# First attention of a fused mLSTM-attention and fp4 feed-forward kernel: the next unit's second score half and state sums issued ahead of this unit's values

## The chip, the cores and the metric

The kernel runs on one core of a Trainium2 chip. The metric is the device time of one execution in microseconds. Before the change it is 559.58 us, the median of 3 runs (558.65 to 561.35).

## What is computed

An attention with gated decay (mLSTM) and a residual, then a feed-forward layer with fp4 weights and a residual, on x of 8 batches x 256 tokens x 512 features. Cut to what matters:

```python
# attention, for each of 8 batches and 16 heads of width 32 (q = layernorm(x), k = v = ctx)
ig, fg   = concat(q, k, v) @ Wi + bi, concat(q, k, v) @ Wf + bf      # per token and head
log_D    = tril(cumsum differences of log_sigmoid(fg)) + ig
D        = exp(log_D - rowmax(log_D))
C        = (q @ k.T / sqrt(32)) * D
h        = C / (max(|rowsum(C)|, exp(-rowmax)) + eps) @ v
x        = x + headwise_layernorm(h) * ln_scale

# feed-forward: gate and up 512 -> 2 x 1408, down 1408 -> 512, fp4 weights with scales
y        = silu(ln(x) @ w_gate) * (ln(x) @ w_up) @ w_down
x        = x + y / rms(y)
```

## The kernel before

The 8 batches are worked in 4 pairs `p`. Attention of pair `p` shares its stretch of the program with the feed-forward layer of pair `p - 1` (`q`). The first pair has no feed-forward beside it (`q is None`); this is **the first attention**, and in it DVE unpacks the fp4 weights (`decode`, a chain of three operations on DVE) and ACT widens them (`convert`). The first attention is all that the change touches.

Attention of a pair is cut into 8 units (`UNITS`): 4 groups of 4 heads by 2 batches. For unit `u` the work is this:

- ACT, `exps(p, u, half)`: 8 exponentials write the decay matrix `dmat[:, u % 2]`. They wait for `pv_done` of unit u - 2, since that unit's values have read the same buffer.
- POOL, `mask(p, u)`: two triangular selects on `dmat`, one for each half of the exponentials, then two small products that write `vw[:, u % 2]` (values weighted by the last row's decay) and count `vw_ready`.
- PE, `scores(p, q, u, 0)` and `(..., 1)`: q k.T in two halves, into banks of `pq` for even units and of `pf` for odd ones.
- PE, `state_sums`: one product of the context with `vw`, the state that the first 128 tokens hand to the later 128. It waits for `vw_ready` of its unit.
- DVE, `products`: scores times `dmat`, in place. It waits for the whole scores, the mask and `vw`. Then `keep_state` copies the state sums out.
- PE, `values(p, q, u)`: 8 small products of `dmat` with `v_sb` into `po`, then one product of `state` with the queries into the second part of bank `pq[:, 1]`, which counts `pv_done`.
- ACT `read_o` copies `po` out, DVE `later_part` scales the part that came from the state, and `add_later` adds it.

In the first attention PE also runs identity matmuls of 128x512 that nothing reads, `keep_busy(count)`, beside its units.

Each engine has a program of its own, written as a loop over 22 steps `h`, and runs it strictly in order. What sets the order is a table: unit u has its scores step at h = 2u + 1 and its values step at h = 2u + 2. At the values step of unit u PE runs, in the first attention, `scores(u + 1, 0)`, `keep_busy`, `values(u)`, `scores(u + 1, 1)`, `state_sums(u + 1)`, `keep_busy`. On ACT, step 2u + 3 holds `read_o(u)` and then `exps(u + 2)`; on POOL it holds `mask(u + 2)`.

After the last unit come the head norm, the first residual and the second layer norm, mostly one chain on DVE, and then the feed-forward layer of the first pair.

Semaphore waits are written ahead of the operation that they guard, as `pe.wait_ge(...)`; everything behind such a wait on that engine waits too.

Of the kernel before, what the change touches and what calls it, by code (L numbers as in the profile page):

```python
# [32 lines left out]
P = 128  # L33
B, S, E, NH = 8, 256, 512, 16
DH = E // NH
# [3 lines left out]
HG = P // DH  # L39
# [70 lines left out]
def xattn_ffn(nc, x, ctx, ctxT, w_gates, b_gates, ln_scale, gu_bytes, gu_scales, dn_bytes, dn_scales, out):  # L110
# [7 lines left out]
    with es:  # L118
# [98 lines left out]

        def bank_qk(p, u, half):
            return pf[:, 2 * half] if p == 0 and u % 2 else pq[:, 2 * half]

        def bank_y(p, n):
            return po[:] if n == 2 else pq[:, min(n, 2)]
# [573 lines left out]
        def _(pe):  # L796
# [71 lines left out]
            def state_sums(p, q, u):  # L868

                hg, b = u // 2, u % 2  # L870
                pe.wait_ge(vw_ready, 2 * UNITS * p + 2 * u + 2)
                if u > 0:
                    pe.wait_ge(later_ready, UNITS * p + u)
                elif q is not None:
                    pe.wait_ge(t_ready, 4 * FT * q + 2)
                pe.matmul(pq[:, 1, 0:HG * (DH + 1)], ctx_sb[:, 2 * b, hg * P:(hg + 1) * P],  # L876
                          vw[:, u % 2].rearrange("q h d -> q (h d)"), start=True, stop=True
                          ).then_inc(st_done, 1)

            def values(p, q, u):  # L880
                hg, b = u // 2, u % 2
                if u == 0 and q is not None:
                    pe.wait_ge(acc_ready, 4 * FT * q + 2)
                if u == 0:
                    pe.wait_ge(v_ready, TT * p + TT)
                if u > 0:
                    pe.wait_ge(o_read, UNITS * p + u)
                elif not (isinstance(p, int) and p == 0):
                    pe.wait_ge(o_read, UNITS * p)
                for half in range(2):  # L890

                    pe.wait_ge(prod_done, 2 * UNITS * p + 2 * u + 1 + half)
                    for s in range(BLKS):
                        for hh in range(2):
                            h = 2 * half + hh
                            pe.matmul(po[:, (s * HG + h) * (DH + 1):(s * HG + h + 1) * (DH + 1)],  # L896
                                      dmat[:, u % 2, half, s, hh], v_sb[:, 2 * b + s, hg * HG + h],
                                      start=True, stop=True)

                pe.wait_ge(state_ready, UNITS * p + u + 1)  # L900
                pe.matmul(pq[:, 1, HG * (DH + 1):2 * HG * (DH + 1)], xT[:, hg, b * S + P:(b + 1) * S],  # L901
                          state[:, u % 2].rearrange("q h d -> q (h d)"), start=True, stop=True
                          ).then_inc(pv_done, 1)
# [73 lines left out]
            def keep_busy(count):  # L977

                words = ident[:].bitcast(F16)
                for _ in range(count):  # L980
                    pe.matmul(pf[:, 3], words[:, 0:P], words.unsqueeze(1).to_broadcast([P, 2, 2 * P]),  # L981
                              start=True, stop=True)

            def iteration(p, q, n):
                for h in range(GU):
                    if q is not None:
                        ffn_up(q, h)
                    if p is not None:

                        s = slot(q, h)  # L990
                        if q is None and s in VALUES and VALUES[s] + 1 < UNITS:
                            scores(p, q, VALUES[s] + 1, 0)
                            keep_busy(6 if VALUES[s] == 0 else 3)
                        if s in VALUES:
                            values(p, q, VALUES[s])
                            if q is None and VALUES[s] + 1 < UNITS:
                                scores(p, q, VALUES[s] + 1, 1)
                                state_sums(p, q, VALUES[s] + 1)
                                keep_busy(6 if VALUES[s] == 0 else 3)
                        if s in SCORES and (q is not None or SCORES[s] == 0):  # L1000
                            scores(p, q, SCORES[s], 0)
                            if q is None:
                                keep_busy(16)
                            state_sums(p, q, SCORES[s])
                            scores(p, q, SCORES[s], 1)
                if q is not None:
                    down(q, 0, range(FT))
                    down(q, 1, range(FT))
                if n is not None:
                    if q is None:  # L1010
                        keep_busy(16)
                    turn_x(n)
                    gate_sums(n)
                    if q is None:
                        keep_busy(36)
                if q is not None:
                    down(q, 2, range(FT))
                if p is not None:
                    turn_y(p)
                if q is not None:  # L1020
                    down(q, 3, range(FT - 3))
                if n is not None:
                    turn_back(n)
                if q is not None:
                    down(q, 3, range(FT - 3, FT))
# [14 lines left out]
        def _(dve):  # L1040
# [87 lines left out]

            def keep_state(p, u):
                dve.wait_ge(st_done, UNITS * p + u + 1)  # L1130
                dve.tensor_tensor(state[:, u % 2], pq[:, 1, 0:HG * (DH + 1)].rearrange(
                    "q (h d) -> q h d", h=HG), own_rows[:], ALU.mult).then_inc(state_ready, 1)

            def later_part(p, u):
# [155 lines left out]
            def iteration(p, q, n):  # L1290
                for h in range(GU):
                    s = slot(q, h)
                    u = SCORES.get(s) if p is not None else None
                    if u is not None and q is None:
                        products(p, u, range(BLKS))
                        keep_state(p, u)
                    if q is not None:
                        ffn_up(q, h, p, u)
                        if q == 0 and h % 2 == 0:
                            down_weights(h // 2)  # L1300
                        if h % 2 == 1 and h > 1:
                            gate(q, h // 2 - 1)
                    elif h in WORDS_AT:
                        i = WORDS_AT[h]
                        decode_up(i) if i < UP_CHUNKS else decode_down(i - UP_CHUNKS)
                    if p is not None and s in VALUES:
                        later_part(p, VALUES[s])
                    if p is not None and s in ADD:
                        add_later(p, ADD[s])
                    if q is None and 11 <= h < 11 + TT:  # L1310
                        norm1_sums(n, (h - 11,))
                    if q is None and h == 11 + TT:
                        shift1(n)
# [97 lines left out]
```

## Time and profile before

| | us |
|---|---|
| median of 3 runs | 559.58 |
| lowest and highest | 558.65, 561.35 |
| the profiled execution, device time | 560.9 |
| its span, first to last instruction | 559.2 |
| PE busy in the span | 504.4 (90%) |
| DVE busy | 391.4 (70%) |
| POOL busy | 331.9 (59%) |
| ACT busy | 295.6 (53%) |

The span is 1.7 us shorter than the device time of that execution. The eight units of the first attention lie between about 42 and 89 us of the span. The values of unit 0 begin at 45.05 us and those of units 1 to 7 at 52.69, 57.81, 62.93, 68.05, 73.17, 78.96 and 84.46 us; the last product of unit 7 ends at 88.57 us. Times in timelines are counted from the start of the span. The granted clock of TensorE is shown as a share of full speed: 1.00 is 2.4 GHz and 0.50 is 1.2 GHz.

### The profile page before, as it was taken

To read this page: it belongs to the slowest core of one execution; us is meant where nothing else is said; L and a number is where in the kernel's file an instruction comes from. 1 tells how busy PE (TensorE), PEld (TensorE's weight loads), DVE (VectorE), ACT (ScalarE), POOL (GpSimd) and SP (SyncE) were. 2 spreads that over 40 slices of the span, in tenths; PEclk is the share of its full clock that TensorE was granted. 3 is DMA by queue.
4 is the path that set the end of the run, shared out by engine and by line. 5 is a ranking of instruction groups with operands and counts; after the bars stand their busy time and mean duration, and the time that the engine had idled before them with its cause. 6 is when DMAs were issued, how large, how long until landed. Compare 5 with 4: busy or idle time off the path is not lost.

```text
span 559.2 us, 8167 instructions
## 1 busy us (share of the span) xinstructions
PE 504.4 (90%) x2728; PEld 279.4 (50%) x2728; DVE 391.4 (70%) x691; ACT 295.6 (53%) x639; POOL 331.9 (59%) x371
## 2 busy tenths in 40 slices
PE   0449989968999899999999999999999989988996
PEld 0326765425666444456665445466664443322442
DVE  4675886985888897647777899377778962877301
ACT  0335765275777623377786354577766123866000
POOL 1043533457888685466777783767777662888501
PEclk9868996988999999999999999999999999999999
DMA  8654309164200600166006000653000000200000
GB/s 254 174 156 186 114 2 320 38 227 151 77 1 2 226 1 1 42 222 240 28 2 226 1 0 4 198 212 119 2 0 2 19 20 19 94 1 1 19 20 38
DMA packets 22218, 48.33 MB, mean 86 GB/s; under 512 B 1824, under 2 KB 8864, under 8 KB 21536
## 3 DMA queue, kind: packets, MB, share of 16 engines
q1 hardware_dynamic: 22176, 47.81, 25.4%
q8 instruction: 22, 0.36, 0.3%
q14 instruction: 20, 0.16, 0.1%
HBM read 37.84 MB, written 4.33 MB: 75 GB/s over the span
## 4 chain that ended last, share of the span: by engine, by line
PE 68%; DVE 14%; issue 5%; ACT 4%; POOL 4%; DMA 4%; SPq 1%; DVEq 0%; POOLq 0%; ACTq 0%
PE pf L972 25%; PE pf L958 17%; PE po L896 9%; PE pq L864 6%; PE pq L876 2%; DMA ts<-in_gate_up_bytes 2%; DVE ffn L1221 2%; PE pq L958 2%; PE pq L901 2%; ACT dmat L648 2%; PE pf L981 2%; DVE ffn L1225 1%; PE pq L826 1%; POOL hT L530 1%; ACT ts L682 1%
## 5 line engine op out<-in xcount | busy, mean ns | idle before, releaser
L972 PE MATMUL pf<-w_down,hT 128*128 128x512 f32 x352 | 154.1, 595 | 1.7 <-DVE w_down L1287 1.7
L958 PE MATMUL pf<-yT,gu_val 128*128 128x512 f16 x552 | 135.6, 385 | 4.2 <-ACT th L707 1.5
L525 POOL TENSOR_TENSOR ffn<-ffn,ts 128x512 f32<-128x512 f32 x88 | 117.6, 1337 | 31.9 <-DVE ffn L1225 22.1
L682 ACT ACTIVATE ts<-pf,gu_scale 128x512 f32<-128x512 f32 x138 | 87.5, 684 | 51.1 <-PE pf L958 50.8
L972 PEld LDWEIGHTS pf<-w_down,hT 128*128 128x128 f32 x352 | 65.9, 190 | 83.7 <-issue 77.1
L958 PEld LDWEIGHTS pf<-yT,gu_val 128*128 128x128 f16 x552 | 50.7, 99 | 68.7 <-DVE ffn L1225 8.2
L648 ACT ACTIVATE dmat<-negm,aT 128x128 f32<-128x128 f32 x256 | 80.0, 395 | 4.9 <-DMA negm<-negm_dram 4.9
L530 POOL TENSOR_TENSOR hT<-ffn,th 128x512 f32<-128x512 f32 x44 | 57.6, 1313 | 30.9 <-DVE th L1234 30.9
L1221 DVE SCALAR_TENSOR_TENSOR ffn<-pf,gu_scale,ts 128x512 f32<-128x512 f32 x69 | 51.6, 748 | 33.7 <-PE pf L958 20.0
L896 PEld LDWEIGHTS po<-v_sb,dmat 128*128 128x128 f32 x512 | 64.2, 197 | 5.3 <-issue 0.9
L486 POOL TENSOR_SCALAR_AFFINE_SELECT dmat<-dmat 128x512 f32<-128x512 f32 x64 | 44.2, 704 | 30.7 <-ACT dmat L648 30.7
L896 PE MATMUL po<-v_sb,dmat 128*128 128x33 f32 x512 | 61.8, 276 | 0.0
L1225 DVE SCALAR_TENSOR_TENSOR ffn<-pf,gu_scale,ffn 128x512 f32<-128x512 f32 x69 | 51.8, 751 | 8.7 <-PE pf L958 1.0
L1126 DVE SCALAR_TENSOR_TENSOR dmat<-pq,dmat 128x512 f32<-128x512 f32 x56 | 36.1, 686 | 19.5 <-PE pq L864 19.5
L700 ACT ACTIVATE th<-pf 128x512 f32<-128x512 f32 x16 | 9.5, 592 | 72.7 <-PE pf L972 72.7
L864 PE MATMUL pq<-xT 32*128 32x128 f32 x448 | 40.8, 300 | 0.7 <-ACT decay L631 0.7
L536 POOL TENSOR_SCALAR ms<-ssq 128x1 f32<-128x1 f32 x16 | 3.5, 221 | 61.2 <-ACT th L700 60.7
L864 PEld LDWEIGHTS pq<-xT 32*128 32x128 f32 x448 | 30.0, 189 | 16.2 <-issue 11.9
L476 POOL TENSOR_TENSOR v_sb<-ctx_sb,vmean 128x512 f32<-128x512 f32 x16 | 17.9, 1152 | 32.7 <-DVE negm L1111 21.3
L1234 DVE SCALAR_TENSOR_TENSOR th<-th,ffn 128x512 f32<-128x512 f32 x44 | 33.9, 779 | 0.0
L981 PE MATMUL pf<-ident 128*128 128x512 f16 x116 | 33.5, 437 | 0.0
L691 ACT ACTIVATE th<-ffn 128x512 f32<-128x512 f32 x44 | 27.9, 635 | 8.4 <-POOL ffn L525 8.4
(118 smaller groups left out, 634.0 us busy)
## 6 DMA issues: line engine op xcount, KB each, us to landing
negm<-negm_dram SPq DMA_DIRECT2D x32, 512.0 KB, 5.3
ffn<-in_x SPq DMA_DIRECT2D x4, 1024.0 KB, 7.5
xT<-in_ctx_T SPq DMA_DIRECT2D x16, 256.0 KB, 5.8
ctx_sb<-in_ctx SPq DMA_DIRECT2D x4, 1024.0 KB, 5.4
x_sb<-in_x SPq DMA_DIRECT2D x4, 1024.0 KB, 5.2
x_res<-x_sb SPq DMA_DIRECT2D x4, 1024.0 KB, 5.3
out<-x_res SPq DMA_DIRECT2D x16, 256.0 KB, 2.1
ts<-in_gate_up_bytes SPq DMA_DIRECT2D x2, 704.0 KB, 11.8
```

The costliest lines, as they stand in the source:

```text
L486: pool.affine_select(out=d, in_=d, compare_op=ALU.is_ge, fill=0.0, base=0, pattern=[[0, HG], [1, P]], channel_multiplier=-1).then_inc(mask ...
L525: pool.tensor_tensor(acc, acc, ts[:, h % TDEEP, 1], ALU.add).then_inc(tsum_ready, 1)
L530: pool.tensor_tensor(hT[:, j], ffn[:, 6 + j % 2], th[:, j % 2], ALU.mult).then_inc(h_ready, 1)
L648: last = act.activation(dmat[:, u % 2, half, c, hh], negm[:, u % 4, h, c * P:(c + 1) * P], ACT.Exp, bias=aT[:, c, bh:bh + 1])
L682: act.activation(ts[:, h % TDEEP, g], bank(q, h, g), ACT.Copy, scale=gu_scale[:, g * GU + o:g * GU + o + 1]).then_inc(t_ready, 1)
L864: last = pe.matmul(bank_qk(p, u, half)[:, c:c + P], xT[r, KT + hg, t0:t0 + P], xT[r, hg, t0:t0 + P], start=True, stop=True)
L896: pe.matmul(po[:, (s * HG + h) * (DH + 1):(s * HG + h + 1) * (DH + 1)], dmat[:, u % 2, half, s, hh], v_sb[:, 2 * b + s, hg * HG + h], star ...
L958: last = pe.matmul(bank(q, h, g), gu_val[:, h // 2 + h % 2 * FT, g], yT[:, part, g], start=(part == 0), stop=(part == 1))
L972: last = pe.matmul(pf[:, tt], hT[:, j, tt * P:(tt + 1) * P], w_down[:, j], start=(j == 0), stop=(j == FT - 1))
L981: pe.matmul(pf[:, 3], words[:, 0:P], words.unsqueeze(1).to_broadcast([P, 2, 2 * P]), start=True, stop=True)
L1221: dve.scalar_tensor_tensor(acc, bank(q, h, 2), gu_scale[:, 2 * GU + o:2 * GU + o + 1], ts[:, h % TDEEP, 0], ALU.mult, ALU.add).then_inc(ac ...
L1225: dve.scalar_tensor_tensor(acc, bank(q, h, 3), gu_scale[:, 3 * GU + o:3 * GU + o + 1], acc, ALU.mult, ALU.add).then_inc(acc_ready, 1)
```

## The change

At the values step of unit u in the first attention, PE runs `scores(u + 1, 0)`, `state_sums(u + 1)`, `scores(u + 1, 1)`, `keep_busy`, and only then `values(u)`. One of the two `keep_busy` groups of each step is gone: 6 identity matmuls for unit 0 and 3 for each of units 1 to 6. The state sums of the first attention go to bank `pf[:, 1]`, so that they wait for the copy of the sums before them (`state_ready`) in place of `later_ready`, and the wait for `later_ready` moves to the last product of `values`. DVE runs `later_part(u - 1)` after `products(u)` and `keep_state(u)`; before, it ran ahead of them.

```diff
@@ bank_state
+        def bank_state(p):
+            return pf[:, 1] if p == 0 else pq[:, 1]
@@ state_sums
                 pe.wait_ge(vw_ready, 2 * UNITS * p + 2 * u + 2)
-                if u > 0:
+                if p == 0:
+                    if u > 0:
+                        pe.wait_ge(state_ready, u)
+                elif u > 0:
                     pe.wait_ge(later_ready, UNITS * p + u)
                 elif q is not None:
                     pe.wait_ge(t_ready, 4 * FT * q + 2)
-                pe.matmul(pq[:, 1, 0:HG * (DH + 1)], ctx_sb[:, 2 * b, hg * P:(hg + 1) * P],
+                pe.matmul(bank_state(p)[:, 0:HG * (DH + 1)], ctx_sb[:, 2 * b, hg * P:(hg + 1) * P],
@@ values
+                if p == 0 and u > 0:
+                    pe.wait_ge(later_ready, u)
                 pe.wait_ge(state_ready, UNITS * p + u + 1)
@@ PE iteration
                         if q is None and s in VALUES and VALUES[s] + 1 < UNITS:
                             scores(p, q, VALUES[s] + 1, 0)
+                            state_sums(p, q, VALUES[s] + 1)
+                            scores(p, q, VALUES[s] + 1, 1)
                             keep_busy(6 if VALUES[s] == 0 else 3)
                         if s in VALUES:
                             values(p, q, VALUES[s])
-                            if q is None and VALUES[s] + 1 < UNITS:
-                                scores(p, q, VALUES[s] + 1, 1)
-                                state_sums(p, q, VALUES[s] + 1)
-                                keep_busy(6 if VALUES[s] == 0 else 3)
@@ keep_state
-                dve.tensor_tensor(state[:, u % 2], pq[:, 1, 0:HG * (DH + 1)].rearrange(
+                dve.tensor_tensor(state[:, u % 2], bank_state(p)[:, 0:HG * (DH + 1)].rearrange(
@@ DVE iteration
                     if u is not None and q is None:
                         products(p, u, range(BLKS))
                         keep_state(p, u)
+                        if u > 0:
+                            later_part(p, u - 1)
+                    if q is None and s - 1 in VALUES and VALUES[s - 1] == UNITS - 1:
+                        later_part(p, UNITS - 1)
@@
-                    if p is not None and s in VALUES:
+                    if p is not None and q is not None and s in VALUES:
                         later_part(p, VALUES[s])
```

How the order moves, on the two engines that matter. PE at the values step of unit 1, before (L864 the scores, L981 the identity matmuls, L896 the small products of `values`, L901 its product with the state, L876 the state sums; the names after the form are the semaphores waited for):

```order
L864 MATMUL pq<-xT 128x128 [waits prod_done,xT_read]
L864 MATMUL pq<-xT 128x128 x3
L981 MATMUL pf<-ident 128x512 x3
L896 MATMUL po<-v_sb,dmat 128x33 [waits prod_done,o_read]
L896 MATMUL po<-v_sb,dmat 128x33 x3
L896 MATMUL po<-v_sb,dmat 128x33 [waits prod_done]
L896 MATMUL po<-v_sb,dmat 128x33 x3
L901 MATMUL pq<-state,xT 128x132 [waits state_ready]
L864 MATMUL pq<-xT 128x128 [waits qk_half]
L864 MATMUL pq<-xT 128x128 x3
L876 MATMUL pq<-vw,ctx_sb 128x132 [waits later_ready,vw_ready]
L981 MATMUL pf<-ident 128x512 x3
```

The same step after (L867 the scores, L882 the state sums, L989 the identity matmuls, L902 and L909 the values):

```order
L867 MATMUL pq<-xT 128x128 [waits prod_done,xT_read]
L867 MATMUL pq<-xT 128x128 x3
L882 MATMUL pf<-vw,ctx_sb 128x132 [waits state_ready,vw_ready]
L867 MATMUL pq<-xT 128x128 [waits qk_half]
L867 MATMUL pq<-xT 128x128 x3
L989 MATMUL pf<-ident 128x512 x3
L902 MATMUL po<-v_sb,dmat 128x33 [waits prod_done,o_read]
L902 MATMUL po<-v_sb,dmat 128x33 x3
L902 MATMUL po<-v_sb,dmat 128x33 [waits prod_done]
L902 MATMUL po<-v_sb,dmat 128x33 x3
L909 MATMUL pq<-state,xT 128x132 [waits state_ready,later_ready]
```

The row that waits for `vw_ready` (of unit 2 here) stood behind the values of unit 1 and now stands ahead of them.

DVE from the copy of unit 0's state sums on, before (L1131 `keep_state`, L1254 to L1256 the decode, L1139 `later_part`, L1126 `products`, L1149 `add_later`):

```order
L1131 TENSOR_TENSOR state<-pq,own_rows 128x132 [waits st_done]
L1254 TENSOR_SCALAR yT<-ts,shifts 128x704
L1255 TENSOR_SCALAR yT<-yT 128x704 [waits dve_w]
L1256 SCALAR_TENSOR_TENSOR hT<-yT 128x22x32 [waits dve_w]
L1139 TENSOR_TENSOR later<-pq,decay 128x132 [waits dve_w,floor_ready,pv_done]
L1126 SCALAR_TENSOR_TENSOR dmat<-pf,dmat 128x512 [waits qk_done,vw_ready,mask_done]
L1126 SCALAR_TENSOR_TENSOR dmat<-pf,dmat 128x512
L1131 TENSOR_TENSOR state<-pq,own_rows 128x132 [waits st_done]
```

and after (the same operations at L1137, L1260 to L1262, L1145, L1132, L1155):

```order
L1137 TENSOR_TENSOR state<-pf,own_rows 128x132 [waits st_done]
L1260 TENSOR_SCALAR yT<-ts,shifts 128x704
L1261 TENSOR_SCALAR yT<-yT 128x704 [waits dve_w]
L1262 SCALAR_TENSOR_TENSOR hT<-yT 128x22x32 [waits dve_w]
L1132 SCALAR_TENSOR_TENSOR dmat<-pf,dmat 128x512 [waits dve_w,qk_done,vw_ready,mask_done]
L1132 SCALAR_TENSOR_TENSOR dmat<-pf,dmat 128x512
L1137 TENSOR_TENSOR state<-pf,own_rows 128x132 [waits st_done]
L1145 TENSOR_TENSOR later<-pq,decay 128x132 [waits floor_ready,pv_done]
L1260 TENSOR_SCALAR yT<-ts,shifts 128x704
L1261 TENSOR_SCALAR yT<-yT 128x704 [waits dve_w]
```

`later_part`, the row that waits for `pv_done`, went from ahead of the next unit's products to behind them, and ahead of the next decode.

ACT, POOL and the DMA queue keep their order.

## Rows read from the trace of the kernel before

**Rows 1.** The page, its first part: busy time, share and instructions of each engine.

```profile
PE 504.4 (90%) x2728; PEld 279.4 (50%) x2728; DVE 391.4 (70%) x691; ACT 295.6 (53%) x639; POOL 331.9 (59%) x371
```

**Rows 2.** Waits of PE from 44 to 89 us: total, times, longest.

```profile
PE pq L876 <- DVE later L1139: 1.6, 3, 0.8
```

**Rows 3.** Timeline of PE, one unit: start, us, engine, line, operation, count, idle before.

```profile
57.81 1.87 PE L896 MATMUL po<-v_sb,dmat 128*128 128x33 f32 x16
59.51 0.47 PE L901 MATMUL pq<-state,xT 128*128 128x132 f32 x2
59.91 0.71 PE L864 MATMUL pf<-xT 32*128 32x128 f32 x8
60.56 0.49 PE L876 MATMUL pq<-vw,ctx_sb 128*128 128x132 f32 x2
60.89 0.81 PE L981 MATMUL pf<-ident 128*128 128x512 f16 x3
61.63 0.71 PE L864 MATMUL pq<-xT 32*128 32x128 f32 x8
62.27 0.82 PE L981 MATMUL pf<-ident 128*128 128x512 f16 x3
62.93 1.87 PE L896 MATMUL po<-v_sb,dmat 128*128 128x33 f32 x16
```

**Rows 4.** Timeline of ACT behind the values of unit 2.

```profile
60.02 0.39 ACT L655 ACTIVATE tok<-po 128x264 f32<-128x264 f32 x1 [1.14 <-PE pq L901]
60.31 2.43 ACT L648 ACTIVATE dmat<-negm,aT 128x128 f32<-128x128 f32 x8
```

**Rows 5.** Timeline of POOL: mask and `vw` of unit 1, then of unit 4.

```profile
43.78 0.63 POOL L486 TENSOR_SCALAR_AFFINE_SELECT dmat<-dmat 128x512 f32<-128x512 f32 x1 [0.53 <-ACT dmat L648]
44.38 0.55 POOL L495 TENSOR_TENSOR vw<-v_sb,dmat 128x66 f32<-128x66 f32 x2
...
62.90 0.91 POOL L486 TENSOR_SCALAR_AFFINE_SELECT dmat<-dmat 128x512 f32<-128x512 f32 x1 [0.53 <-ACT dmat L648]
63.78 1.18 POOL L495 TENSOR_TENSOR vw<-v_sb,dmat 128x66 f32<-128x66 f32 x2
```

**Rows 6.** Timeline of DVE: `keep_state` of unit 0, and a decode of unit 3's step.

```profile
45.14 0.28 DVE L1131 TENSOR_TENSOR state<-pq,own_rows 128x132 f32<-128x132 f32 x1
...
62.18 0.58 DVE L1254 TENSOR_SCALAR yT<-x_res,shifts 128x704 int32<-128x704 int32 x1
...
63.35 1.20 DVE L1256 SCALAR_TENSOR_TENSOR ts<-yT 128x704 int32<-128x704 int32 x1
```

**Rows 7.** Timeline of PE around units 0 and 1, and unit 0's last product.

```profile
43.75 1.47 PE L981 MATMUL pf<-ident 128*128 128x512 f16 x6
...
46.76 0.47 PE L901 MATMUL pq<-state,xT 128*128 128x132 f32 x2
...
48.37 2.76 PE L981 MATMUL pf<-ident 128*128 128x512 f16 x6
```

**Rows 8.** Busy time by stretch: stretch, length, PE, PEld, DVE, ACT, POOL, PEclk, DMA, GB/s.

```profile
82.50:84.00 1.50, 1.40 (x4) 0.84 (x5) 1.32 (x4) 0.33 (x1) 0.33 (x1) 0.50 0.00 0
84.00:86.00 2.00, 2.00 (x10) 1.66 (x8) 1.30 (x5) 0.74 (x1) 0.69 (x1) 0.50 0.38 128
90.00:92.00 2.00, 2.00 (x6) 0.76 (x5) 1.56 (x1) 2.00 (x4) 1.51 (x2) 0.50 0.96 309
```

**Rows 9.** Timeline of PE: scores of unit 0, then the end of the units.

```profile
33.98 1.23 PE L864 MATMUL pq<-xT 32*128 32x128 f32 x8 [0.69 <-ACT decay L631]
...
82.60 0.78 PE L876 MATMUL pq<-vw,ctx_sb 128*128 128x132 f32 x2 [0.82 <-DVE later L1139]
83.18 1.49 PE L981 MATMUL pf<-ident 128*128 128x512 f16 x3
84.46 3.51 PE L896 MATMUL po<-v_sb,dmat 128*128 128x33 f32 x16
87.78 0.79 PE L901 MATMUL pq<-state,xT 128*128 128x132 f32 x2
```

**Rows 10.** The chain that ended last, behind the units: start, us, what.

```profile
88.60 0.40 ACT tok L655
...
90.44 2.29 DVE hn L1154
```

## The prediction, made before the changed kernel ran

> **What bounds the kernel now.** Over the whole span PE is busy for 504.4 of 559.2 us [rows 1], but the change touches only the first attention, so I read that stretch alone, 42 to 89 us. First the waits of PE: from 44 to 89 us it waited only 1.6 us in all [rows 2]. So PE sets the pace there. Then the timeline of PE for one unit: the values of unit 2 begin at 57.81 and those of unit 3 at 62.93 us, a period of 5.12 us without a gap [rows 3]. From start to start it is made of the values' small products 1.70, the product with the state 0.40, a score half 0.65, the state sums 0.33, three identity matmuls 0.74, the other score half 0.64 and three more identity matmuls 0.66. The identity matmuls are 1.40 us of it, and it is they that the change halves.
>
> Then I followed the other engines from the end of one unit's values, because that is where exponentials start. The product with the state of unit 2 ends at 59.51 + 0.47 = 59.98 us [rows 3]. ACT copies `po` at 60.02 and runs the 8 exponentials of unit 4 from 60.31 to 62.74 us [rows 4]; POOL's second mask of unit 4 begins at 62.90 and its two `vw` products end at 63.78 + 1.18 = 64.96 us [rows 5]. I call this the **side leg**: 4.98 us from `pv_done` of unit u to `vw_ready` of unit u + 2. Before the change it runs beside a whole period of PE, since PE wants `vw` of unit u + 2 only behind the values of unit u + 1. It costs nothing now.
>
> **The change part by part.**
>
> *Removed: identity matmuls.* 6 for unit 0 and 3 for each of units 1 to 6. At full clock 3 of them cost 0.66 to 0.74 us and 6 cost 1.47 us [rows 3, 7], so 6 x 0.7 + 1.4 = 5.6 us of PE at most. They are worth that only if PE stays the bound.
>
> *Removed: the wait for `later_ready` ahead of the state sums,* 1.6 us in all [rows 2]. The wait that goes to the last product of `values` is met long before, as `later_part` of the unit before runs right behind its `pv_done`.
>
> *Moved: `state_sums(u + 1)` ahead of `values(u)` on PE.* This is the part that decides. The state sums wait for `vw_ready` of unit u + 1. `vw` of that unit needs its exponentials, and these wait for `pv_done` of unit u - 1, since both units share a buffer. PE runs in order, so behind the waiting state sums stand the second score half, the identity matmuls and the whole of `values(u)`, and for `pv_done` of unit u in turn ACT waits. Before, the loop was: values of u - 1, side leg, values of u + 1, which is two units for each side leg. Now it is: values of u - 1, side leg, values of u. One unit for each side leg, and PE has no work but one score half while the leg runs. The double buffer of `dmat` and `vw` no longer hides anything.
>
> The loop, step by step. The side leg first. In the new order DVE decodes directly behind `later_part`, which is at the start of the leg, and is done with its three operations some 2.5 us into it; before, the decode at 62.18 to 64.55 us [rows 6] lay on the second mask and on `vw`. Without a decode beside them the mask took 0.60 to the start of `vw` and `vw` 0.55 [rows 5], against 0.88 and 1.18 with it. So the leg is 62.90 - 59.98 = 2.92, + 0.60 + 0.55 = 4.07 us at its shortest and 4.98 at its longest. I take 4.15, near the short end, because the new place of the decode is the early one. To it comes 0.05 us until the state sums start, an estimate from the 0.04 us between the end of PE's product and ACT's start [rows 3, 4].
>
> On the shared port the Trainium skill ("SBUF — State Buffer", section "SBUF: two separate sides") says that DVE and GpSimd hold a pair of ports exclusively, for a whole instruction, and the other blocks. The trace agrees, with `vw` at 0.55 alone and 1.18 us beside a decode. By that rule with the decode's old place the leg would stay 4.98 us and the sum below would be 5 us larger.
>
> Then PE's part of the loop: state sums, a score half, three identity matmuls, values, product with the state.
> - At full clock: 0.33 + 0.65 + 0.66 + 1.70 + 0.47 = 3.81 us [rows 3]. The loop is 4.15 + 0.05 + 3.81 = 8.0 us.
> - At half clock: state sums 0.58 (82.60 to 83.18), scores 1.2 (from 1.23 at 33.98), identity matmuls 1.28 (83.18 to 84.46), values 3.32 (84.46 to 87.78), state product 0.79 [rows 9], together 7.17 us. The loop is 4.15 + 0.05 + 7.17 = 11.37 us.
>
> Which clock? From 82.5 us on the granted clock is 0.50 [rows 8], that is 1.2 GHz, behind a wait of only 0.82 us [rows 9], and it was still 0.50 at 90 to 92 us although PE had been without a gap since 82.60. In that stretch PE ran the state sums, three identity matmuls and the values, the very same mix as the new loop, and only after many more identity matmuls did it come back. In the new loop PE stands still for 3 to 3.5 us of every unit (the leg less one score half) and has half as many identity matmuls. So I take the half clock for all of it, from the end of unit 0 on.
>
> *The first unit.* `state_sums(1)` now waits for `keep_state(0)`, which ends at 45.14 + 0.28 = 45.42 us [rows 6]; `vw` of unit 1 is ready at 44.93 [rows 5]. So it starts at about 45.5, and with 0.33 + 0.65 + 1.4 (six identity matmuls) + 1.70 + 0.47 unit 0 ends at 50.0 us; before, it ended at 46.76 + 0.47 = 47.23 [rows 7]. The cost is 2.8 us.
>
> *The sum.* `state_sums` of units 2 to 7 each wait for a side leg, so 6 loops: unit 6 ends at 50.0 + 6 x 11.37 = 118.2 us. Unit 7's values have their products ready and wait only for the copy of `po`, 0.45 us, and take 3.32 + 0.79: unit 7 ends at 122.8 us, where before it ended at 87.78 + 0.79 = 88.57 [rows 9]. The difference is **+34.2 us**. At full clock throughout it would be 50.0 + 6 x 8.0 + 0.45 + 1.70 + 0.47 = 100.6, **+12.0 us**. The removed identity matmuls are in these sums, since only the ones that are left are counted; their 5.6 us bring nothing, because PE waits for POOL.
>
> *What lies behind.* The chain goes on from the last `pv_done` through the copy of `po` and the head sums on DVE [rows 10] and nothing in it is changed, so the shift is passed on in full. The unpacking of weights keeps up with the slower units: DVE and ACT get more idle time, not less. The loads for the next pair are released by counts that come no later against the end of unit 7 than before. All other attentions keep their order and waits. Everything else: 0.
>
> The profiled execution took 560.9 us, 1.3 above the median; the change is a shift of one stretch, so I add it to the median: 559.6 + 34 = 593.6, taken as 593.5 us.
>
> **The rivals.**
>
> *The clock returns inside every burst.* The six identity matmuls at 48.37 us took 2.76 us against 1.47 for the six at 43.75, that is half clock, and a unit later everything runs at full rate again [rows 3, 7]. If in each burst the clock is half for the first three parts (0.58 + 1.2 + 1.28 = 3.06 us) and full for the values (1.70 + 0.47), the loop is 4.20 + 3.06 + 2.17 = 9.43 us, unit 6 ends at 106.6 and unit 7 at 109.2: +20.6, 580.2 us. For it speaks [rows 7]; against it that those were six identity matmuls in a row and here there are three among others, and that the same three at 83.18 did not bring the clock back [rows 8, 9]. The Trainium skill ("TensorE: Matmul & The Clock Gate", section "What's actually happening") says that the throttled state is the default and activity releases it, which by itself would let a burst recover; the trace shows both outcomes. 0.17, mixtures among them.
>
> *Full clock throughout,* 571.6 us. Against it: the clock fell behind gaps shorter than these. 0.06.
>
> *A longer stretch than summed:* the leg at 4.98 us (+5.0), or unit 0's burst at half clock too (+2 to 3). 598 to 601 us. 0.07 beyond 600.
>
> *Not slower.* It would need `vw` of unit u + 1 to be ready when PE gets to its state sums, right behind the values of u - 1. The place is the wait of `exps(u + 1)` for `pv_done` of u - 1: if that leg took under about 1.3 us (5.12 - 3.81), the loop would be shorter than the old period, and with 0.7 us saved in each of 7 steps and no stretch at half clock at the end (1.9 us on unit 7's values) the kernel would come to about 552 us. The leg holds 8 exponentials of 2.43 us alone, so the point is far away. 0.02 for this, and 0.02 that the order does not bite for a reason I don't see and the time stays.
>
> **How the numbers follow.** Half clock as summed 0.66, recovery inside bursts 0.17, longer 0.07, full clock 0.06, same 0.02, faster 0.02. The predicted time is the first case, 593.5 us. The range goes from 577, which takes in the recovery case with a little more of full clock, to 601, the long leg with a slow first burst; it leaves out about 0.12. A measurement of this kernel tells about 0.5% (2.8 us) from no change: slower by more than that 0.96, within it 0.02, faster 0.02.
>
> **What would show it.** In the timeline after, the state sums of units 2 to 7 on PE should each stand behind a wait of 3 us or more with POOL's `vw` as releaser, and units should begin 11 us apart (8 at full clock). The granted clock from about 52 us to the end of the units should be near 0.5. The masks should be 0.6 us and `vw` near 0.55, if the decode has left them alone. From the end of unit 7 on, the distances should be as before: 1.9 us to the head sums. The forecast is wrong in sign if PE shows no such wait, and wrong in size if the clock in that stretch is near 1.

## The result, and the profile after

The changed kernel takes 594.88 us (median of 4 runs, 592.62 to 596.89) against 559.12 us for the kernel before, measured beside it (4 runs, 555.32 to 561.35). The ratio is 1.0646, 95% interval 1.0575 to 1.0717: slower, inside the range of 577 to 601 us and 1.4 us above the forecast. The ratios here leave out executions more than 1.5% above the fastest of the same kernel, which show a lower mean granted clock.

| | before | after |
|---|---|---|
| span of the profiled execution, us | 559.2 | 593.7 |
| PE busy | 504.4 (90%) | 523.3 (88%) |
| mean granted clock | 0.967 | 0.918 |
| last product of unit 7 ends at, us | 88.57 | 122.95 |
| from there to the end of the span | 470.6 | 470.8 |

The last two rows say where the time went: in this pair of executions all of it into the eight units of the first attention, with nothing gained or lost behind them. The page of the profile after shows the stretch as a hollow in PE's tenths from the fourth slice on, with the clock at 5 (each slice is 14.8 us):

```profile
PE 523.3 (88%) x2704; PEld 295.8 (50%) x2704; DVE 391.0 (66%) x691; ACT 295.9 (50%) x639; POOL 330.5 (56%) x371
...
PE   0567767797699998999999999999999998988996
...
PEclk9976555579889999999999999999999999999999
```

The waits of PE and its loads of weights from 44 to 124 us (total, times, longest), where [rows 2] showed 1.6 us for `later_part` alone:

```profile
PE pf L882 <- POOL vw L498: 18.4, 6, 3.5
...
PE pf L882 <- DVE state L1137: 1.8, 1, 1.8
```

Six waits of the state sums for `vw`, for units 2 to 7. One period in PE's timeline, to be held against [rows 3] and [rows 9] (L882 state sums, L867 scores, L989 identity matmuls, L902 and L909 values):

```profile
60.75 0.79 PE L909 MATMUL pq<-state,xT 128*128 128x132 f32 x2
61.47 1.23 PE L867 MATMUL pf<-xT 32*128 32x128 f32 x8
65.67 0.81 PE L882 MATMUL pf<-vw,ctx_sb 128*128 128x132 f32 x2 [2.98 <-POOL vw L498]
66.41 1.23 PE L867 MATMUL pf<-xT 32*128 32x128 f32 x8
67.56 1.46 PE L989 MATMUL pf<-ident 128*128 128x512 f16 x3
68.81 3.46 PE L902 MATMUL po<-v_sb,dmat 128*128 128x33 f32 x16
72.09 0.79 PE L909 MATMUL pq<-state,xT 128*128 128x132 f32 x2
```

From product with the state to product with the state it is 72.09 - 60.75 = 11.34 us, where [rows 3] had 5.12. From the product of unit 1 (60.75 us) to that of unit 6 (117.45) every step is 11.34 us; the one from unit 0 to unit 1 is 11.03, since unit 0 ended at full clock. The chain that ended last walks through exactly the leg of the prediction (start, us, what):

```profile
60.94 0.61 PE pq L909 x2
...
61.57 0.04 ACT tok L658
...
61.86 1.27 ACT dmat L651 x4
...
63.29 1.05 POOL dmat L489
...
64.46 0.64 POOL dmat L489
65.09 0.53 POOL vw L498 x2
65.62 0.04 issue
65.67 0.81 PE pf L882 x2
```

PE ends the product at 61.54 us, `vw` is there at 65.62: a side leg of 4.08 us. And the busy time by stretch (stretch, length, PE, PEld, DVE, ACT, POOL, PEclk, DMA, GB/s) shows PE busy for 8.37 of 11 us, at 1.2 GHz:

```profile
52.00:63.00 11.00, 8.37 (x39) 6.73 (x39) 3.97 (x9) 3.65 (x10) 2.17 (x4) 0.50 0.15 48
```

### The profile page after: what moved, and what is told of

Same layout as the page of the kernel before. It is cut to its first block, busy times and chain, and to the rows that moved or that the text cites. A ratio compares the mean times of both kernels' runs of the same rounds, so it can differ in the third digit from the quotient of the medians.

```text
span 593.7 us, 8126 instructions
## 1 busy us (share of the span) xinstructions
PE 523.3 (88%) x2704; PEld 295.8 (50%) x2704; DVE 391.0 (66%) x691; ACT 295.9 (50%) x639; POOL 330.5 (56%) x371
## 4 chain that ended last, share of the span: by engine, by line
PE 69%; DVE 11%; POOL 6%; ACT 5%; issue 5%; DMA 3%; SPq 1%; POOLq 0%; DVEq 0%; ACTq 0%
PE pf L980 23%; PE pf L966 16%; PE po L902 11%; PE pq L867 6%; ACT dmat L651 3%; POOL dmat L489 2%; DMA ts<-in_gate_up_bytes 2%; PE pq L909 2%; PE pf L989 2%; DVE ffn L1227 2%; PE pq L882 2%; PE pq L966 2%; DVE ffn L1231 1%; PE pq L829 1%; POOL hT L533 1%
## 5 line engine op out<-in xcount | busy, mean ns | idle before, releaser
L489 POOL TENSOR_SCALAR_AFFINE_SELECT dmat<-dmat 128x512 f32<-128x512 f32 x64 | 46.0, 734 | 64.2 <-ACT dmat L651 63.6
L902 PEld LDWEIGHTS po<-v_sb,dmat 128*128 128x128 f32 x512 | 75.2, 225 | 7.0 <-issue 2.2
L902 PE MATMUL po<-v_sb,dmat 128*128 128x33 f32 x512 | 71.9, 301 | 0.5 <-ACT tok L658 0.5
L1132 DVE SCALAR_TENSOR_TENSOR dmat<-pq,dmat 128x512 f32<-128x512 f32 x56 | 36.1, 686 | 25.4 <-PE pq L867 25.4
L867 PE MATMUL pq<-xT 32*128 32x128 f32 x448 | 43.0, 313 | 0.7 <-ACT decay L634 0.7
L867 PEld LDWEIGHTS pq<-xT 32*128 32x128 f32 x448 | 31.7, 199 | 15.5 <-issue 11.4
L658 ACT ACTIVATE tok<-po 128x264 f32<-128x264 f32 x32 | 12.5, 391 | 53.0 <-PE pq L909 53.0
```

Source lines behind the costliest of these rows:

```text
L489: pool.affine_select(out=d, in_=d, compare_op=ALU.is_ge, fill=0.0, base=0, pattern=[[0, HG], [1, P]], channel_multiplier=-1).then_inc(mask ...
L867: last = pe.matmul(bank_qk(p, u, half)[:, c:c + P], xT[r, KT + hg, t0:t0 + P], xT[r, hg, t0:t0 + P], start=True, stop=True)
L1132: dve.scalar_tensor_tensor(d, bank_qk(p, u, half), float(DH) ** -0.5, d, ALU.mult, ALU.mult).then_inc(prod_done, 1)
```

## The experiments

Two things could make the 34 us, and they are entangled in the changed kernel: PE's wait for `vw` in every unit, and the half clock. The clock in turn could fall because of the waits or because of the identity matmuls that were removed. The runs were chosen to separate these. They were measured in three groups, each on one chip and with the kernel before beside them (medians 558.3, 557.9 and 560.5 us).

### Undoing the order alone

```diff
                             scores(p, q, VALUES[s] + 1, 0)
-                            state_sums(p, q, VALUES[s] + 1)
-                            scores(p, q, VALUES[s] + 1, 1)
                             keep_busy(6 if VALUES[s] == 0 else 3)
                         if s in VALUES:
                             values(p, q, VALUES[s])
+                            if q is None and VALUES[s] + 1 < UNITS:
+                                scores(p, q, VALUES[s] + 1, 1)
+                                state_sums(p, q, VALUES[s] + 1)
```

> The changed kernel with PE's order of before (values of unit u, then the second score half and the state sums of unit u + 1), all else as changed: own bank, one group of identity matmuls, later_part behind the next products. If the order is the cause, the 3 to 3.5 us waits of the state sums for POOL's vw go (under 0.5 us each) and the units come at most 5.1 us apart at full clock: 4.4 us of PE work each, 553 to 560 us. If the missing identity matmuls alone pull the clock down, the units are 8.4 us apart at half clock, about 580 us. If the bank or the order on DVE were the cause, it stays near 594.

The four times were 555.3, 568.9, 570.7 and 574.5 us, so the median of 569.8 hides a spread, and no ratio is given; neither branch of the expectation, 553 to 560 or about 580 us, holds for all four. The trace of the one at 570.7 us has no wait of the state sums for `vw`, but the half clock:

```profile
51.53 0.79 PE L909 MATMUL pq<-state,xT 128*128 128x132 f32 x2
52.24 1.23 PE L867 MATMUL pq<-xT 32*128 32x128 f32 x8
53.40 0.81 PE L882 MATMUL pf<-vw,ctx_sb 128*128 128x132 f32 x2
54.14 1.23 PE L867 MATMUL pf<-xT 32*128 32x128 f32 x8
55.30 1.46 PE L989 MATMUL pf<-ident 128*128 128x512 f16 x3
56.55 3.46 PE L902 MATMUL po<-v_sb,dmat 128*128 128x33 f32 x16
59.82 0.79 PE L909 MATMUL pq<-state,xT 128*128 128x132 f32 x2
```

Units are 8.29 us apart, all of it PE's work at 1.2 GHz. So the order makes the waits, 11.34 - 8.29 = 3.05 us of each unit, and the half clock does not need them. The one execution at 555.3 us has no trace, but its mean granted clock is on record: 0.970, where the other three have 0.930 to 0.940 and the kernel before beside them 0.965 to 0.973. So the clock held in that one, or fell for a short while only: with three identity matmuls per unit it does not fall every time.

### Taking the identity matmuls away alone

```diff
                                 scores(p, q, VALUES[s] + 1, 1)
                                 state_sums(p, q, VALUES[s] + 1)
-                                keep_busy(6 if VALUES[s] == 0 else 3)
```

from the kernel before.

> The kernel before with nothing changed but the second group of identity matmuls taken away (6 and six times 3). If the clock holds, each unit loses 0.66 us: 554 to 556 us. If the clock needs them, PE's unit goes from 5.1 to some 8 us at half clock and the time to 575 to 585 us. The prediction assumed for the new loop that half as many identity matmuls do not hold the clock, with idle time beside; this run has no idle time.

569.74 us, ratio 1.0209 (1.0171 to 1.0246), and a mean granted clock of 0.935 to 0.949 in all four executions. The time lies below the 575 to 585 expected for a lost clock. Work that nothing reads was removed from a PE that was the bound, and the kernel got 11.8 us slower. The busy time by stretch (columns as above) shows the clock go, with PE busy almost throughout (7.81 of the first 8 us, then without a gap):

```profile
42.00:50.00 8.00, 7.81 (x77) 6.28 (x69) 7.04 (x13) 5.45 (x12) 3.06 (x6) 1.00 0.50 197
50.00:53.00 3.00, 3.00 (x24) 2.03 (x24) 2.57 (x7) 2.45 (x9) 1.50 (x3) 0.82 0.34 137
53.00:60.00 7.00, 7.00 (x34) 6.04 (x34) 3.71 (x7) 3.84 (x10) 2.65 (x4) 0.50 0.67 207
60.00:90.00 30.00, 30.00 (x144) 24.43 (x141) 18.24 (x36) 13.64 (x33) 11.24 (x16) 0.50 0.02 6
```

PE is busy for 30.00 of 30 us at 0.50. The kernel before, with six identity matmuls per unit in place of three, is busy for 29.16 us of the 30 from 52 to 82 and has 1.00 throughout. So a share of busy time does not say which clock is granted. Units are 8.29 us apart here too.

### Giving them back to the changed kernel

```diff
                             scores(p, q, VALUES[s] + 1, 0)
+                            keep_busy(6 if VALUES[s] == 0 else 3)
                             state_sums(p, q, VALUES[s] + 1)
```

> The changed kernel with the removed group of identity matmuls back in its old place, behind the first score half (so it lies in the wait for vw). Order as the cause: the wait shrinks by 1.3 us, nothing is gained, units 11.3 us apart if the clock stays at half, 594 us (8.0 us apart and 573 us only if these few matmuls hold the clock). Removed identity matmuls as the whole cause: back to 559 us.

595.09 us, 1.0639 (1.0565 to 1.0713): no gain at all. The group lies in the wait, which shrinks from 2.98 to 1.58 us, and the units stay 11.34 us apart (the state sums of units 3 and 4 below start 74.17 - 62.83 us apart):

```profile
62.83 0.81 PE L882 MATMUL pf<-vw,ctx_sb 128*128 128x132 f32 x2 [1.58 <-POOL vw L498]
...
74.17 0.81 PE L882 MATMUL pf<-vw,ctx_sb 128*128 128x132 f32 x2 [1.58 <-POOL vw L498]
```

So each fault is enough by itself to bring the half clock: fewer identity matmuls without a wait, or the wait with as many identity matmuls as before.

### Filling the wait until the clock holds

```diff
                             scores(p, q, VALUES[s] + 1, 0)
+                            keep_busy(12)
                             state_sums(p, q, VALUES[s] + 1)
```

> The changed kernel with 12 identity matmuls behind the first score half, which fill the wait for vw (2.6 us at full clock). It prices the clock apart from the wait. Order and clock as in the prediction: clock back at 1, units 8.0 us apart, 570 to 573 us, so 21 to 24 us of the 34 are the clock and 12 the wait. If the clock is not what doubles PE's part, it stays at 594 or gets slower.

576.03 us, 1.0304 (1.0244 to 1.0365). The clock is 1.00 in every stretch and only the wait is left:

```profile
53.45 0.49 PE L882 MATMUL pf<-vw,ctx_sb 128*128 128x132 f32 x2 [0.79 <-POOL vw L498]
...
61.48 0.49 PE L882 MATMUL pf<-vw,ctx_sb 128*128 128x132 f32 x2 [0.79 <-POOL vw L498]
...
100.14 5.26 PE L989 MATMUL pf<-ident 128*128 128x512 f16 x16
```

Units are 61.48 - 53.45 = 8.03 us apart, where the prediction's sum at full clock had 8.0. The identity matmuls behind unit 7 begin at 100.14 us; in the kernel before they begin at 88.36. These 11.8 us are the wait's share of the shift, and the 22.6 from there to the changed kernel's 122.73 are the clock's. The whole time came out 3 us above the expected 570 to 573; from the last product of unit 7 to the end of the span it is 472.8 us here, 2.1 more than in the kernel before.

### Shortening the side leg

```diff
+                    if p == 0:
+                        last = act.activation(dmat[:, u % 2, half, :, hh],
+                                              negm[:, u % 4, h].rearrange("q (c s) -> q c s", c=BLKS),
+                                              ACT.Exp, bias=aT[:, 0, bh:bh + 1])
+                        continue
                     for c in range(BLKS):
```

> The changed kernel with 4 exponentials of 256 columns for each unit of the first attention in place of 8 of 128 (the second block of columns takes the bias of the first, so part of the decay matrix is not computed as it should be). It shortens the side leg alone, by an estimated 0.5 to 1.0 us. If the leg is in the loop of every unit, the units come closer by the whole of it, 6 times: 3 to 6 us less, 588 to 591 us. If the leg is hidden, nothing moves: 594 us.

This kernel leaves out the second block's own bias and uses that of the first, so it serves for its time alone. 596.24 us, 1.067 (1.0599 to 1.0741): nothing gained in the whole. The exponentials did shrink, from 2.43 to 1.69 us, but POOL's timeline shows where most of it went:

```profile
64.56 0.63 POOL L489 TENSOR_SCALAR_AFFINE_SELECT dmat<-dmat 128x512 f32<-128x512 f32 x1 [8.65 <-ACT dmat L651]
65.35 1.08 POOL L489 TENSOR_SCALAR_AFFINE_SELECT dmat<-dmat 128x512 f32<-128x512 f32 x1 [0.16 <-ACT dmat L651]
66.40 0.59 POOL L498 TENSOR_TENSOR vw<-v_sb,dmat 128x66 f32<-128x66 f32 x2
```

The second mask came 0.7 us earlier and so onto the decode's third operation on DVE, and took 1.08 in place of 0.64 us. The loop shrank by what was left, from 11.34 to 11.08 us (state sums at 67.05, 78.12, 89.20 and 100.28 us). In six loops that is 1.6 us, and it was paid back in unit 0, whose values ran at half clock throughout here (3.46 us from 48.03 us on, where the changed kernel had 2.39 from 47.49), 1.6 us together. The step "the leg is in the loop of every unit" holds at this small size; the expected 3 to 6 us do not, because the price of the exponentials was taken without the slower mask beside DVE's decode.

### The state sums last, the early score half kept

```diff
                             scores(p, q, VALUES[s] + 1, 0)
-                            state_sums(p, q, VALUES[s] + 1)
                             scores(p, q, VALUES[s] + 1, 1)
                             keep_busy(6 if VALUES[s] == 0 else 3)
                         if s in VALUES:
                             values(p, q, VALUES[s])
+                            if q is None and VALUES[s] + 1 < UNITS:
+                                state_sums(p, q, VALUES[s] + 1)
```

and the same with `keep_busy(6 if VALUES[s] == 0 else 3)` behind the state sums.

> The changed kernel with only the state sums put back behind the values; both score halves stay ahead of the values, one group of identity matmuls. The order theory in its narrow form says that the wait for vw in the state sums is the whole fault and the early score half is harmless: no wait above 0.5 us on PE, units 4.4 to 5.1 us apart at full clock, 553 to 560 us. If the early score half itself were at fault, the units stay 8 us or more apart, 570 us or more.

> As the one with the state sums last, but with the second group of identity matmuls behind them, as many as before the change. PE work of a unit is again 5.1 us: 557 to 560 us, clock 1. Beside its sister with one group it shows what the second group costs or holds up.

With one group 566.12 us, 1.0122 (1.0055 to 1.0188), in neither branch of the expectation. The four executions go from 561.1 to 575.4 us with a mean clock from 0.954 down to 0.929. The profiled one is the slowest: no wait for `vw`, but units 8.1 us apart at half clock; the others have no trace. With two groups 560.60 us, 1.0021 (0.9981 to 1.0061), units 5.06 us apart at full clock; nine of ten executions lie at 556.4 to 563.6 us, and one at 587.1 with a mean clock of 0.917, without a trace:

```profile
60.80 1.87 PE L902 MATMUL po<-v_sb,dmat 128*128 128x33 f32 x16
...
65.86 1.87 PE L902 MATMUL po<-v_sb,dmat 128*128 128x33 f32 x16
```

So with both groups there the early score half, the own bank and the new order on DVE cost nothing that these times show, and of the two things that moved ahead of the values on PE the state sums are the one that hurts.

### A third buffer

If the loop is closed by the buffer that units u + 1 and u - 1 share, a third one must open it with the changed order left as it is. The decay matrix of units 2 and 5 goes to `th`, their `vw` to a part of `ffn`, both idle in the first attention, the exponentials wait for one unit less and run ahead of `read_o`:

```diff
+        def dm(p, u):
+            if p == 0 and u % 3 == 2:
+                return th[:].rearrange("q a b -> q (a b)").rearrange(
+                    "q (f c h s) -> q f c h s", f=2, c=BLKS, h=HG // 2)
+            return dmat[:, u % 3 if p == 0 else u % 2]
...
-                    if u >= 2:
+                    if p == 0:
+                        if u >= 3:
+                            act.wait_ge(pv_done, u - 2)
+                    elif u >= 2:
```

> The changed kernel, all in its new order, with a third buffer for the decay matrix and vw in the first attention (in tiles that are idle then), so that exponentials of unit u + 1 wait for the values of unit u - 2 and not u - 1; ACT runs them ahead of the copy of po. If the shared buffer is what closes the loop, the side leg is hidden again: no wait of the state sums above 0.5 us, units 4.4 to 5 us apart, 553 to 560 us. If something else holds the state sums, the units stay 8 to 11 us apart.

575.40 us, 1.0349 (1.0298 to 1.04). The wait is gone: from 44 to 98 us nothing on PE waits for POOL (the state sums of unit 3 follow the score half directly), and the units are again 8.29 us apart at half clock:

```profile
56.12 1.23 PE L882 MATMUL pf<-xT 32*128 32x128 f32 x8
57.28 0.81 PE L897 MATMUL pf<-vw,ctx_sb 128*128 128x132 f32 x2
...
65.57 0.81 PE L897 MATMUL pf<-vw,ctx_sb 128*128 128x132 f32 x2
```

The shared buffer as the cause of the wait is shown. The order on ACT changed with it, but that could take away little: in the chain of the changed kernel the exponentials start 0.28 us behind the copy of `po`, and the wait was 2.98. The expected 553 to 560 us are not reached; the expectation left out the second fault, the missing identity matmuls. With both mended:

```diff
                             scores(p, q, VALUES[s] + 1, 0)
+                            keep_busy(6 if VALUES[s] == 0 else 3)
                             state_sums(p, q, VALUES[s] + 1)
```

> The changed kernel with both of its faults mended and nothing of its order undone: the third buffer, which takes the wait for vw away, and the second group of identity matmuls, back behind the first score half, for the clock. Units 5.1 us apart at full clock without waits, 555 to 560 us. If the early state sums cost something beside these two, it stays above 565.

557.28 us over 12 runs against 560.47 for the kernel before, ratio 0.9944 (0.9907 to 0.998): the lowest median of all, 6% below the changed kernel and 0.6% below the one before. The last is small beside what else moves: the kernel before had medians of 557.9 to 560.5 us in the three groups, and the filled kernel below has 558.01. One of the 12 lies at 570.0 us, with a mean clock of 0.950. From unit 0 to unit 6 the values begin 5.03 to 5.09 us apart, at full clock and with no wait; unit 7 waits 1.5 us for its products, and its last part runs at half clock:

```profile
55.58 1.87 PE L917 MATMUL po<-v_sb,th 128*128 128x33 f32 x16
...
58.33 0.82 PE L1004 MATMUL pf<-ident 128*128 128x512 f16 x3
58.99 0.39 PE L897 MATMUL pf<-vw,ctx_sb 128*128 128x132 f32 x2
...
60.61 0.64 PE L917 MATMUL po<-v_sb,dmat 128*128 128x33 f32 x5
```

### How many identity matmuls, and where

Six in one group ahead of the values (`keep_busy(12 if VALUES[s] == 0 else 6)`, with the state sums last); groups of 2 in place of 3 in the kernel before; and 3 more ahead of the state sums of units 6 and 7 in the kernel before, in its two waits.

> The kernel with the score halves ahead of the values and the state sums behind them, with as many identity matmuls as before the change but all in one group ahead of the values (12 for unit 0, then 6). If their number is what holds the clock, 557 to 561 us, as with two groups. If it is that they come twice in each unit, the clock falls and the units are 8.1 + 1.3 us apart, about 575 us.

> The kernel before with groups of 2 identity matmuls for units 1 to 6 in place of 3, in both places: 4 for each unit, between the 6 of before and the 3 of the change. If 4 hold the clock, each unit is 0.45 us shorter, 555 to 557 us. If not, the units are some 8.7 us apart at half clock, 570 to 578 us.

> The kernel before with 3 identity matmuls more ahead of the state sums of units 6 and 7, where PE waited 0.6 and 0.8 us for later_part and behind which the clock fell at 82.5 us. They cost nothing if they lie in the waits. If they hold the clock, the values of unit 7 take 1.9 and not 3.5 us: 555 to 557 us. Else 558 to 559.

One group of six: 560.30 us, 1.001 (0.9968 to 1.0052). The time is as expected if the number counts, but the trace shows units 5.06 us apart up to 60 us and 6.6 to 6.7 afterwards, without a wait, and the clock at a mean of 0.83 from 56 to 78 us. In the trace of the same order with two groups it was 1.00 there. So the place matters beside the number as far as these two executions go; the whole times, 560.30 and 560.60 us, don't tell them apart. Groups of two: 560.29 us, 0.9992 (0.995 to 1.0035), between the two times expected; units 4.7 and 4.9 us apart in turn, as hoped, until the clock falls ahead of unit 6:

```profile
72.43 0.46 PE L876 MATMUL pq<-vw,ctx_sb 128*128 128x132 f32 x2 [0.86 <-DVE later L1139]
...
75.24 3.46 PE L896 MATMUL po<-v_sb,dmat 128*128 128x33 f32 x16
```

What four per unit gain early is lost late. Whether four are too few is not shown: the fall comes behind a wait of 0.86 us, as it came behind one of 0.82 in the kernel before with six.

The filled waits: 558.01 us, 0.9957 (0.9915 to 1.0), not told apart from no change. Seven of the 12 executions took 554.1 to 558.8 us with a mean clock of 0.974 to 0.985, five took 562.0 to 567.8 with 0.961 to 0.970. The profiled one, 562.7, is of the slower five, so its trace does not stand for the kernel. In it the clock held to the end of the units, and the values of unit 7 took 1.94 in place of 3.51 us. The identity matmuls behind the units begin at 83.05 us, 5.3 earlier than in the kernel before; yet this execution spans 560.9 us against 559.2. The loss is in the start of the second attention. There the mean granted clock was 0.54 from 130 to 133.5 us and near 1.00 around it in the kernel before, and 0.50 from 124 to 137 us here, nearly four times as long. PE was busy, so 9.5 us more at half clock cost some 4.7 us, an estimate:

```profile
124.05 0.81 PE L876 MATMUL pq<-vw,ctx_sb 128*128 128x132 f32 x2 [2.17 <-POOL vw L495]
...
125.94 3.59 PE L958 MATMUL pf<-yT,gu_val 128*128 128x512 f16 x8
129.33 3.46 PE L896 MATMUL po<-v_sb,dmat 128*128 128x33 f32 x16
...
133.18 3.62 PE L958 MATMUL pf<-yT,gu_val 128*128 128x512 f16 x8
```

The same eight `L958` take 1.89 us at full clock. By the first product of the down projection (193.51 us here, 193.59 before) all 5.3 us were gone. In the 35 executions of the kernel before in this group time and mean clock go together: 556.0 and 556.4 us at 0.982, all those above 563 us at 0.960 to 0.967. So the clock, behind the units too, is likely what spreads the times of every kernel here over 5 us and more. That was not tested by itself, and in which stretches it falls is known for the traced executions alone.

## Why the prediction was right

**What bounds the kernel now:** right. With the state sums back behind the values, and two groups, the units are 5.06 us apart, where the kernel before had 5.12.

**The state sums ahead of the values close a loop of one unit:** right, as the term that decides. Six waits for `vw`, of 3.49 and five times 2.98 us, and the third buffer takes them away.

**The side leg, taken at 4.15 us between 4.07 and 4.98:** measured 4.08. The decode did move off `vw` (0.53 us in the chain, where [rows 5] had 1.18 beside a decode), and onto the first mask (1.05 in place of 0.63), where the second exponentials cover it. The shortened leg of the experiment shows the other side: a mask that comes early meets the decode. Both agree with the Trainium skill on the shared port ("SBUF — State Buffer", "SBUF: two separate sides"), as the prediction cited it.

**PE's part at half clock, 7.17 us:** measured 72.09 + 0.79 - 65.67 = 7.21. The loop was 11.34 against 11.37 us, and unit 7 ended at 122.95 against 122.8.

**The first unit, 50.0 us:** it ended at 49.72 + 0.47 = 50.19, but by luck: two errors met. The state sums began at 44.00 and not 45.5, since unit 0 came 1.5 us earlier in this execution, ahead of anything the change touches. And the clock fell already in this burst, so the six identity matmuls took 2.45 to the start of the values in place of 1.4, and the values 2.23 in place of 1.70. Without the early start unit 7 would have ended at about 124.5 us, 1.7 later than the sum.

**The clock:** the level was right. The prediction named the idle time in the loop and "half as many identity matmuls" side by side, with the stretch at 82.5 us of [rows 8] for both. The runs divide them: the idle time is one sufficient cause (both groups in place, and still 0.50), and the removed identity matmuls are another, in seven of the eight executions with the old order on PE and one group, by their mean clocks. The step that failed is the sentence that the removed identity matmuls "bring nothing": taken away alone, they cost 11.8 us. It did not change the sum, because the waits bring the half clock by themselves: with the group back in place the changed kernel still took 595.09 us.

**The rival of recovery inside every burst** did not happen in any of the six bursts of units 1 to 6. It did happen in unit 0's, whose six identity matmuls took 2.66 us, most of it at half clock, and whose last product took 0.47, at full clock. The Trainium skill's sentence that activity releases the throttle ("TensorE: Matmul & The Clock Gate", "What's actually happening") does not carry over to this mix of small matmuls: with one group of identity matmuls taken from the kernel before, the clock stayed at 0.50 through 30 us without a gap.

**The split of the sum,** 12 us for the wait and 22 for the clock, was confirmed by the end of the units in the filled kernel (11.8 and 22.6 us). In whole times it is 17.7 and 18.9 us (558.3, 576.0, 594.9), since the stretch behind the units varies by some microseconds.

**What lies behind the units adds nothing:** 470.6 and 470.8 us, right as to the change, but the closeness is luck. In the fourteen traces of this case that stretch goes from 468.9 to 477.6 us, though no edit changes what runs there.

## What to carry to other kernels

Before an instruction is moved ahead of another on an in-order engine, ask what its own wait depends on: here the state sums of unit u + 1 needed a buffer that only the values just ahead of them set free, so the early issue turned a loop of two units for each side leg into one of one. A third buffer took the waits away with the order as it was, and with the second group of identity matmuls back it gave the lowest median of all. So the depth of the buffers has to grow with the lead of the issue. Matmuls that nothing reads can be holding the clock, and whether they do is seen by removing them alone, not together with another change.

## What the runs showed that was not expected

- PE busy for 30.00 of 30 us and still granted 1.2 GHz: with three 128x512 identity matmuls per unit of small products the clock fell from 1.00 to 0.50 in every trace and stayed there (one execution without a trace, at a mean of 0.970, went otherwise). With six in two groups it held at 1.00 while nothing made PE wait. With six in one group it fell at about 63 us, five units in, without a wait, and with four in two groups behind a wait of 0.86 us.
- The wait and the clock add up with little overlap. With three identity matmuls per unit PE's work at full clock would be 5.12 - 0.66 = 4.46 us, an estimate from [rows 3]. The half clock alone gives 8.29, the wait alone 8.03, both 11.34, where 4.46 and the two steps of 3.83 and 3.57 would make 11.86. The 0.5 us between fit the one score half that runs inside the wait, which takes 0.5 us longer at half clock.
- In the one traced execution with the waits filled, a gain of 5.3 us at the end of one stretch was gone in the next, where the clock was at half for longer; the faster executions of that kernel have no trace.
- The mask on POOL went from 0.64 to 1.08 us when it began 0.7 us earlier and met DVE's decode.
